# Last stage of a two-layer transformer kernel: head weights held stationary, new bank and queue orders, and the decay mask applied by GpSimd

## What is computed

```python
def _mlstm_parallel(q, k, v, i_pre, f_pre):            # per block and head
    lf = concatenate([0, cumsum(log_sigmoid(f_pre))])
    log_d = lf[1:, None] - lf[None, 1:] + i_pre[None, :]
    log_d = where(t >= s, log_d, -inf)
    m = max(log_d, axis=-1)
    s_mat = (q @ k.T / sqrt(DH)) * exp(log_d - m)
    denom = maximum(abs(sum(s_mat, -1)), exp(-m)) + 5e-5
    return s_mat @ v / denom
# then per head: h * rsqrt(mean(h*h) + 1e-6) * gain, x = x + h
# second half of the layer, on n = layernorm(x):
gate = softmax(n @ gate_w.T); base = n @ weight.T      # 8 experts, rank 16
out = x + base + (sum over experts of gate * (n @ U) @ V) / 16
```

## Time and profile before

| | us |
|---|---|
| median of 3 runs | 431.02 |
| lowest, highest | 430.0, 435.96 |
| profiled execution, its own time | 433.9 |
| span of the profiled execution | 432.0 |
| mean granted TensorE clock | 0.916 |

### The profile page before, as it was taken

How to read it: one execution, slowest core, us unless ns; L and a number is a source line. 1 busy time by engine, 2 the same in 40 slices (tenths; PEclk the granted TensorE clock), 3 DMA queues, 4 the chain that set the end, 5 groups by cost and what they waited for, 6 DMA issues and landing times.

```text
span 432.0 us, 9170 instructions
## 1 busy us (share of the span) xinstructions
PE 344.1 (80%) x3130; PEld 244.1 (57%) x3137; DVE 306.4 (71%) x1028; ACT 248.9 (58%) x470; POOL 185.1 (43%) x209
## 2 busy tenths in 40 slices
PE   2995698989999999824667776677489999999775
PEld 2774566767677777502445554355356666666422
DVE  3897454778898987676999999951537777787641
ACT  1564424664545545726788988874446666666520
POOL 2115200121212345149999999971004555445520
PEclk9999869999999999955999999989579999999965
DMA  7499999988476540000000000000001122212000
GB/s 242 136 281 281 273 303 289 242 167 150 95 148 112 127 71 2 1 0 0 2 1 2 0 2 1 2 0 2 0 14 27 37 51 50 50 39 39 24 25 24
DMA packets 48045, 35.78 MB, mean 83 GB/s; under 512 B 20096, under 2 KB 44032, under 8 KB 47872
## 3 DMA queue, kind: packets, MB, share of 16 engines
q1 hardware_dynamic: 48000, 35.20, 34.1%
HBM read 26.80 MB, written 8.39 MB: 81 GB/s over the span
## 4 chain that ended last, share of the span: by engine, by line
PE 53%; DVE 17%; issue 12%; ACT 5%; POOL 5%; DMA 3%; SPq 3%; DVEq 0%; POOLq 0%; ACTq 0%
PE PS L1438 6%; PE PS L1227 4%; PE PS L1216 4%; PE PS L1246 4%; DVE sm L736 4%; PE PS L1285 4%; PE PS L1428 4%; PE PS L1207 4%; PE PS L1206 4%; PE PS L1405 3%; DMA scr_k<-kpart 3%; PE PS L1423 2%; ACT pT L990 2%; SPq L315 2%; DVE sm L712 2%
## 5 line engine op out<-in xcount | busy, mean ns | idle before, releaser
L990 ACT ACTIVATE pT<-PS 128x512 f32<-128x512 f32 x64 | 36.6, 596 | 49.5 <-PE PS L1207 49.3
L605 DVE TENSOR_REDUCE negm<-PS 128x4 bf16<-128x512 f32 x64 | 42.4, 684 | 15.5 <-PE PS L1216 15.4
L434 POOL TENSOR_TENSOR sm<-sm,mhalf 128x1 f32<-128x1 f32 x16 | 11.3, 708 | 93.0 <-DVE sm L637 93.0
L450 POOL TENSOR_TENSOR kst<-kst,rows 128x1024 f32<-128x1024 f32 x16 | 37.6, 2351 | 5.0 <-ACT kst L1055 4.9
L464 POOL TENSOR_TENSOR kst<-kst,rows 128x1024 f32<-128x1024 f32 x16 | 37.8, 2365 | 0.0
L1320 PE MATMUL PS<-identf,w2f 128*128 128x128 f32 x128 | 19.2, 298 | 23.2 <-ACT w2f L1044 23.0
L1207 PE MATMUL PS<-identb,negm 128*128 128x128 bf16 x256 | 35.6, 222 | 0.0
L1227 PE MATMUL PS<-pT,vx 128*32 128x128 f32 x512 | 27.3, 287 | 5.0 <-ACT pT L990 5.0
L1320 PEld LDWEIGHTS PS<-identf,w2f 128*128 128x128 f32 x128 | 15.1, 151 | 27.7 <-ACT w2f L1044 22.4
L1438 PE MATMUL PS<-wd,xT 128*128 128x392 f32 x64 | 27.7, 560 | 1.8 <-DVE rest L884 1.8
L484 POOL TENSOR_TENSOR smd<-smd,mhalf 128x1 f32<-128x1 f32 x16 | 8.8, 550 | 44.9 <-DVE smd L915 44.9
(11 more groups left out here) (225 smaller groups left out, 1002.6 us busy)
## 6 DMA issues: line engine op xcount, KB each, us to landing
scr_q<-qpart SPq DMA_DIRECT2D x8, 384.0 KB, 4.9
scr_k<-kpart SPq DMA_DIRECT2D x8, 384.0 KB, 6.0
rows<-in_rows SPq DMA_DIRECT2D x1, 2056.0 KB, 11.3
X<-in_x SPq DMA_DIRECT2D x8, 256.0 KB, 4.7
CTXT<-in_ctxT SPq DMA_DIRECT2D x8, 256.0 KB, 4.6
cTb<-in_ctxT SPq DMA_DIRECT2D x16, 128.0 KB, 4.3
vx<-in_ctx SPq DMA_DIRECT2D x16, 128.0 KB, 2.7
out<-rest SPq DMA_DIRECT2D x16, 128.0 KB, 1.7
```

The lines of the kernel that those rows point to most:

```text
L450: gp.tensor_tensor(n2[q.slot], n2[q.slot], ln2g, ALU.mult).then_inc(b_g2, 1)
L605: v.tensor_reduce(negm[f.slot % 2][:, 4 * hg:4 * hg + 4], PS[:, 2 + hg % 2, :].rearrange("p (h k) -> p h k", h=4), AX_X, ALU.max, negate=T ...
L990: s.activation(pT[:, hg, :], PS[:, hg % 2, :], ACT.Exp, scale=float(DH0) ** -0.5).then_inc(a_e, 1)
```

## The change

It touches the last stage only (and the constant `maskb` that it used).

- TensorE: the product of a head takes `smT` (128x128) as the stationary operand and moves the 33 columns of `vx2`, straight into token-by-value form in bank 6. It moves from block a to block b, that is one turn later, and to the head of the turn. The four transposes and ScalarE's copy `yTc` are gone. The two mask matmuls are gone; the log-decays' 512-column matmul comes first. `nd` is transposed into bank 0, `gt` into bank 1; the low-rank product has half a bank of its own (bank 1, columns 256 to 512).
- The order on TensorE becomes: product (b), transposes of `nd` (e), transpose of `gt` (d), scores (a), product with `wd` (e), low-rank product (d), `log_d(0)`, `log_d(1)` (n). `log_d(1)` waits for the output add of d, since both use bank 1.
- ScalarE: `yc`, `xT`, `hsq`, `gtT`, `nd`, `eD`, then both exps.
- GpSimd: two `affine_select` a turn, in place on `dT`, set the masked decays to zero after the exp; the weights wait for these (`c_k`).
- VectorE: first c (heads, X, statistics), then the norm chain of b in one piece, the weights of a, the gate maximum of e, the output add of d, then reciprocal and `gt` of e and a new add, base = bank 7 + X into `outb` (`d_bs`). The output add then adds the low-rank half bank to `outb`.

```diff
@@ constants on GpSimd
-            step(gp.memset(maskb[:], 0.0))
-            step(gp.affine_select(out=maskb[:], in_=maskb[:], compare_op=ALU.is_ge, fill=-30000.0, base=0,
-                                  pattern=[[1, 128]], channel_multiplier=-1))
@@ GpSimd
+            def turn_cd(n, _a, b, c, _e, _d):
+                def masked(half):
+                    pool.wait_ge(c_d, n.b * 2 + half + 1)
+                    d3 = dT[half].rearrange("p (j t) -> p j t", j=4)
+                    gp.affine_select(out=d3, in_=d3, compare_op=ALU.is_ge, fill=0.0, base=0,
+                                     pattern=[[0, 4], [1, 128]], channel_multiplier=-1).then_inc(c_k, 1)
...
+                if n:
+                    masked(0)
+                    masked(1)
@@ VectorE (the order: c, b, weights(a), then)
-                    dve.wait_ge(c_d, a.b * 2 + n + 1)
+                    dve.wait_ge(c_k, a.b * 2 + n + 1)
...
+                if a:
+                    weights(0)
+                    weights(1)
+                if e:
+                    k2.start(e)
+                    dve.wait_ge(d_m, e.b + 1)
+                    v.tensor_reduce(ngm[:], PS[:, 7, D + ER:NM], AX_X, ALU.max, negate=True).then_inc(d_mx, 1)
                 if d:
...
+                    dve.wait_ge(d_l, d.b + 1)
+                    dve.wait_ge(d_bs, d.b + 1)
+                    v.tensor_tensor(outb[d.slot % 2], PS[:, 1, 256:512], outb[d.slot % 2], ALU.add).then_inc(d_o, 1)
+                if e:
...
+                    v.tensor_tensor(outb[e.slot % 2], PS[:, 7, 0:D], X[:, e.b, :], ALU.add).then_inc(d_bs, 1)
@@ ScalarE (the order: yc, xT, hsq, gtT, nd, eD, exp, exp)
-                    act.wait_ge(c_t4, b.b + 1)
+                    act.wait_ge(c_pv, b.b + 1)
...
-                    s.activation(yTc[:], PS[:, 6, :], ACT.Copy).then_inc(c_yT, 1)
@@ TensorE, log_d
-                    if half == 0:
-                        done(pe, c_y, n, -1)
-                    else:
-                        done(pe, d_xT, n, -3)
+                    if half == 0 and e:
+                        pe.wait_ge(d_xT, e.b + 1)
+                    if half == 1 and d:
+                        pe.wait_ge(d_o, d.b + 1)
...
-                    t.matmul(bank, identb[:], maskb[:].unsqueeze(1).to_broadcast([128, 4, 128]), start=True, stop=False)
+                    t.matmul(bank, APARTS[:, n.used, :], rowsel[:, hs:hs + 4].unsqueeze(2).to_broadcast([128, 4, 128]),
+                             start=True, stop=False)
                     for j in range(4):
...
@@ TensorE, the turn
                 if b:
...
+                    pe.wait_ge(c_ld[b.slot % 2], 16 * (b.b // 2 + 1))
+                    pe.wait_ge(c_sm, b.b * 2 + 2)
+                    done(pe, c_y, b, 0)
+                    for h in range(H1):
+                        last = t.matmul(PS[:, 6, h * (DH1 + 1):(h + 1) * (DH1 + 1)], smT[h // 4][:, (h % 4) * 128:(h % 4 + 1) * 128],
+                                        vx2[b.slot % 2][:, h, 0:DH1 + 1], start=True, stop=True)
+                    last.then_inc(c_pv, 1)
+                if e:
+                    pe.wait_ge(d_n, e.b + 1)
                     exps_read(0)
-                    for i in range(4):
-                        last = t.transpose(PS[:, 0, i * 128:(i + 1) * 128], yTc[:, i * 128:(i + 1) * 128], identf[:])
-                    last.then_inc(c_t4, 1)
+                    for i in range(KC):
+                        last = t.transpose(PS[:, 0, i * 128:(i + 1) * 128], nd[:, i * 128:(i + 1) * 128], identf[:])
+                    last.then_inc(d_t, 1)
+                if d:
+                    pe.wait_ge(d_g, d.b + 1)
+                    exps_read(1)
+                    done(pe, d_o, d, 0)
+                    t.transpose(PS[:, 1, 0:128], gt[:], identf[:]).then_inc(d_gt, 1)
                 if a:
...
                     pe.wait_ge(d_xT, e.b + 1)
-                    done(pe, d_o, e, 0)
+                    done(pe, d_bs, e, 0)
...
+                if d:
+                    pe.wait_ge(d_gT, d.b + 1)
+                    t.matmul(PS[:, 1, 256:512], gtT[:], wlv[:], start=True, stop=True).then_inc(d_l, 1)
+                if n:
+                    log_d(0)
+                    log_d(1)
```

More of the change, by code:

```diff
@@ L239, in build @@
         smT = [lnb[i][:].rearrange("p c t -> p (c t)") for i in range(2)]
-        yTc = sb("yTc", [128, 512]); yc = [sb(f"yc{i}", [128, H1, DH1 + 1]) for i in range(2)]; den = sb("den", [128, H1, 4])
+        yc = [sb(f"yc{i}", [128, H1, DH1 + 1]) for i in range(2)]; den = sb("den", [128, H1, 4])
         hd = [sb(f"hd{i}", [128, D]) for i in range(2)]
@@ L854, in weights @@
                                            op0=ALU.mult, op1=ALU.mult).then_inc(c_sm, 1)
-                if d:
-                    k2.start(d)
-                    dve.wait_ge(d_m, d.b + 1)
-                    v.tensor_reduce(ngm[:], PS[:, 7, D + ER:NM], AX_X, ALU.max, negate=True).then_inc(d_mx, 1)
-                    dve.wait_ge(d_e, d.b + 1)
+                if c:
+                    dve.wait_ge(c_yg, c.b + 1)
+                    dve.wait_ge(c_rr, c.b + 1)
+                    v.tensor_tensor(hv[c.slot % 2], hv[c.slot % 2],
+                                    rr[c.slot % 2][:].unsqueeze(2).to_broadcast([128, H1, DH1]), ALU.mult).then_inc(c_hd, 1)
+                    dve.wait_ge(c_hd, c.b + 1)
+                    v.tensor_tensor(X[:, c.b, :], hd[c.slot % 2][:], X[:, c.b, :], ALU.add).then_inc(c_x, 1)
+                    k1.start(c)
+                    zc = smd[c.slot % 2]
+                    dve.wait_ge(c_x, c.b + 1)
+                    take_wait()
+                    c_bn = k1.mark(v.bn_stats(zc[:, 8:14], X[:, c.b, :]))
+                    dve.wait_ge(d_c1, c_bn)
+                    done(dve, d_r, c, -1)
+                    take_wait()
+                    c_var = k1.mark(v.bn_aggr(zc[:, 0:2], zc[:, 8:14]))
+                    dve.wait_ge(d_c1, c_var)
+                    v.tensor_scalar(zc[:, 4:5], zc[:, 0:1], -1.0, None, ALU.mult)
+                    v.tensor_scalar(zc[:, 2:3], zc[:, 1:2], EPS, None, ALU.add).then_inc(d_w, 1)
+                    k1.end()
@@ new lines, in turn_cd @@
+                if b:
+                    cc.start(b)
+                    yb_l = yc[b.slot % 2][:, :, DH1]
+                    dve.wait_ge(c_y, b.b + 1)
+                    b_neg = cc.mark(v.scalar_tensor_tensor(out=den[:, :, 0], in0=yb_l, scalar=-1.0, in1=EM[:, b.b, :],
+                                                           op0=ALU.mult, op1=ALU.max))
+                    dve.wait_ge(c_ch, b_neg)
+                    b_abs = cc.mark(v.tensor_tensor(den[:, :, 1], den[:, :, 0], yb_l, ALU.max))
+                    dve.wait_ge(c_ch, b_abs)
+                    b_den = cc.mark(v.tensor_scalar(den[:, :, 2], den[:, :, 1], 5e-5, None, ALU.add))
+                    dve.wait_ge(c_sq, b.b + 1)
+                    b_sum = cc.mark(v.tensor_reduce(den[:, :, 0], hsq[b.slot % 2][:].rearrange("p (h e) -> p h e", h=H1),
+                                                    AX_X, ALU.add))
+                    dve.wait_ge(c_ch, b_den)
+                    b_floor = cc.mark(v.scalar_tensor_tensor(out=den[:, :, 3], in0=den[:, :, 2], scalar=1e-6, in1=den[:, :, 2],
+                                                             op0=ALU.mult, op1=ALU.mult))
+                    done(dve, c_rr, b, -1)
+                    dve.wait_ge(c_ch, max(b_sum, b_floor))
+                    v.scalar_tensor_tensor(out=ms[b.slot % 2][:], in0=den[:, :, 0], scalar=1.0 / DH1, in1=den[:, :, 3],
+                                           op0=ALU.mult, op1=ALU.add).then_inc(c_ms, 1)
+                    cc.end()
@@ L1115, in turn_cd @@
                     done(act, d_l, d, 0)
[L1116 to L1124 removed]
+                    s.activation(gtT[:], PS[:, 1, 0:128], ACT.Copy).then_inc(d_gT, 1)
                 if c:
@@ L1129, in turn_cd @@
                                  bias=smd[c.slot % 2][:, 5:6]).then_inc(d_n, 1)
+                if e:
+                    act.wait_ge(d_mx, e.b + 1)
+                    done(act, d_g, e, 0)
+                    s.activation(eD[:], PS[:, 7, D + ER:NM], ACT.Exp, bias=ngm[:], accum_out=esum[:]).then_inc(d_e, 1)
+                if n:
+                    exp(0)
+                    exp(1)
             pipeline(act, NB, 4, 6, turn_cd)
```

130 lines of the change are left out of this document (19 added, 111 removed).

## The result

The changed kernel takes 438.52 us (median of 4 runs, 437.15 to 440.95), the one before 432.72 in the same job (430.0 to 435.96): ratio 1.0126, 95% interval [1.0078, 1.0175]. It is slower by 1.3%, less than the 2% that counts as a difference here, but outside the predicted range of 422.5 to 437, and slower (the interval lies wholly above 1) where 0.8 us less was predicted.

A forecast was written before the change was run, and what follows sets the result against it. TensorE's queue was taken to set the 5.905 us turn, then a loop through all engines. Span 432.0 + 5.2 (turns) - 5.1 (drain) - 0.9 (fill) = 431.2; carried to the median, 430.2 us, range 422.5 to 437.

The forecast's parts named there:

- The turn: Last stage, full turns: 6.38 us instead of 5.905, over eleven turns +5.2 us.
- The loop without holds: Full turn: new loop through all engines, from product to log-decays, takes 5.97 us if GpSimd doesn't hold VectorE.
- the holds: Full turn: GpSimd's select and gain product hold VectorE's add to X and first denominator step, 0.41 us on the loop.
- TensorE's sum: Full turn: TensorE's own work falls from 5.905 to 5.67 us, with the heads' product at 0.11 a pair.
- rival C: Heads' product: weight loads don't hide, 0.138 us a pair, 5.4 us in all, total 435.6; chance 0.12.
- The select: GpSimd, full turn: each 128x512 affine_select takes 0.61 us, hidden as a wait but not as a neighbour of VectorE.
- Rival D: GpSimd's select costs like four small ones, 1.17 us, adding 0.7 a turn, total 438; chance 0.08.
- B: Full turn: GpSimd and VectorE meetings don't cost, turn 5.97 us, total 425.7, or 423 with higher drain clock; chance 0.25.
- A: The main forecast: meetings with GpSimd cost VectorE, turn 6.38 us, total 430.2, own range 427 to 433; chance 0.48.
- The drain: Last turns: low-rank piece leaves the loop and base add enters, 1.7 us saved in each of three turns, -5.1 us.
- The fill: First turn, at the lower clock: two mask matmuls at 0.43 each go, -0.9 us.
- rival E: TensorE's clock falls to 1.2 GHz in full turns, loads alone add 1.76 us a turn, total over 440; chance 0.07.

The follow-up runs named there:

- g_all_dummies: Changed kernel with GpSimd's gain product behind the mean square and unread filler matmuls in TensorE's fill and full turns; ratio 0.9987 to the kernel before.
- g_out_early: Changed kernel with late gain product and filler, plus low-rank product ahead of gate products and output add ahead of weights; ratio 1.0103 to the kernel before.
- x_select_again: Repeat of the kernel before with only the mask products replaced by GpSimd's select; ratio 0.9994 to the kernel before.
- e_all_dummies: Changed kernel with unread filler matmuls in TensorE's waits, five in fill turns and three in full turns; 435.73 us, ratio 1.0066 to the kernel before.
- e_wide64: Changed kernel with each matmul of the heads' product moving 64 columns instead of 33; 439.5 us, ratio 1.0184 to the kernel before.
- e_no_select: Changed kernel without the two selects, the mask left out so its output differs; ratio 1.0063 to the kernel before.
- g_early_bare: Changed kernel with late gain product, low-rank product ahead of gate products, output add ahead of weights, no filler; ratio 1.0138 to the kernel before.
- x_select: Kernel before with only the mask products replaced by GpSimd's select after each exp; ratio 0.9949 to the kernel before.
- x_both: Kernel before, old order, with the select, the low-rank product's own half bank and the base add; ratio 1.0086 to the kernel before.

## Why the prediction was wrong, step by step

**The turn: right, a little short.** 6.48 against 6.38. The loop without holds measured 5.98 against 5.97. The first denominator step was held as said. The term that was short is the holds: 0.50 instead of 0.41 on the loop, since both selects meet VectorE (0.56 for `hd`, 0.79 for the add; I had 0.26 on the add alone). Ten turns of 0.57 are 5.7, with the eleventh 6.3, where I had 5.2.

**TensorE's sum: right within 0.1 us.** 0.109 us a pair against 0.11, so rival C (0.138) is out. In g_all_dummies TensorE has no gap and a turn takes 6.25; less the 0.65 that the same filler took in g_out_early that is 5.60, against 5.67. The Trainium skill ("TensorE: Matmul & The Clock Gate", section "Part 3: Packing small matmuls") would have a full-array load wait for the running matmul; 33 and 64 columns at one pace disagree with it, in this shape.

**The select: right.** 0.61 was said, the mean over all 32 is 0.665. As a wait it is hidden, as a neighbour it isn't. Rival D is out, B too, as the meetings cost what A said. The Trainium skill ("SBUF — State Buffer", section "Who interferes with whom") names the lock; its rule gave 6.38, and the trace agrees within 0.1.

**The drain: the size was right, the reason for the rest wrong.** -7.5 against -5.1. x_select_again drains in the old order at a granted clock of 0.93 and takes 24.6; e_all_dummies in the new one at 0.91 takes 19.9. The order is thus worth 4.7, near 5.1; the other 2.8 come from the clock, 0.72 in the drain of before and 0.88 after. That the total came so near is in part luck: the prediction let the last block's own piece stand, but the last gap between output adds fell from 4.86 to 2.44 us in these two profiles, while the first of the last four grew from 5.61 to 6.26.

**The fill: the step that failed first.** I put down -0.9, for the mask products alone; it was +5.1. With the clock kept (e_all_dummies) +2.0 remain, up to 0.5 of them the filler's own: -0.85 up to the first scores (1.80 us from the first log-decays instead of 2.65, the saving that I had put down), +0.7 and +1.2 in the second and third turn (5.31 and 5.77 against 4.59 and 4.60), +1.05 in the fifth, which is a full one already (6.95 against 5.90). In the second and third run paths that I never walked in the fill. Timeline of e_all_dummies there:

```profile
317.98 0.17 DVE L887 SCALAR_TENSOR_TENSOR den<-yc,EM 128x8 f32<-128x8 f32 x1 [3.02 <-ACT yc L1100]
319.38 0.17 DVE L902 SCALAR_TENSOR_TENSOR ms<-den 128x8 f32<-128x8 f32 x1
319.49 1.29 DVE L856 SCALAR_TENSOR_TENSOR lnb<-PS,lnT 128x512 f32<-128x512 f32 x2
319.64 1.64 POOL L491 TENSOR_TENSOR rr<-ms,mhalf 128x8 f32<-128x8 f32 x1 [0.93 <-DVE ms L902]
321.38 0.78 DVE L865 TENSOR_TENSOR hd<-hd,rr 128x256 f32<-128x256 f32 x1 [0.59 <-POOL rr L491]
322.19 0.73 DVE L868 TENSOR_TENSOR X<-hd,X 128x256 f32<-128x256 f32 x1
322.96 0.42 DVE L873 BATCH_NORM_STATS2 smd<-X 128x6 f32<-128x256 f32 x1
323.77 0.28 DVE L887 SCALAR_TENSOR_TENSOR den<-yc,EM 128x8 f32<-128x8 f32 x1
325.01 1.29 DVE L856 SCALAR_TENSOR_TENSOR lnb<-PS,lnT 128x512 f32<-128x512 f32 x2
```

In the second turn the denominators wait for `yc` (3.02), and the next weights stand behind them: product, `yc`, norm chain and weights, parts of the prediction's loop, take it up. In the third the mean square releases GpSimd's root (1.64), VectorE's multiply waits for it, then come add and statistics, and only behind them, without a wait of their own, the next denominators, mean square and weights. In full turns the gate work of e and d lies in that wait and hides it; in the fill there is none. The old order had the weights ahead of all this.

**The clock: the step that failed by kind.** I gave rival E 0.07 because the new product "leaves TensorE occupied" for 5.67 of 6.38 us, and looked at full turns alone. The rows show it falling at 322.0, in the fill, after TensorE had waited 1.72 us for the weights (they end at 321.17), and again at 383.4, after a wait of 1.07 us, longer than the usual 0.72:

```profile
321.27 2.93 PE L1394 MATMUL PS<-vx,lnb 128*128 128x33 f32 x16 [1.72 <-issue]
...
327.57 3.60 PE L1394 MATMUL PS<-vx,lnb 128*128 128x33 f32 x16 [0.38 <-issue]
...
381.72 0.38 PE L1378 MATMUL PS<-rowsel,APARTS 128*128 128x512 bf16 x1 [1.07 <-DVE rest L915]
...
386.33 2.98 PE L1420 MATMUL PS<-wd,xT 128*128 128x392 f32 x4
```

At 1.2 GHz the product takes 3.60 instead of 1.92, as the loads double, and the four gate products 2.98 instead of 1.58. The two turns around 383.4 took 7.62 and 8.26: with 6.48 for each that is 2.9 too much. Rival E named the right thing, but not its place and size: the clock fell for one stretch of the fill and one of the middle, not for all turns.

**The sum again.** By order: fill +2.0, middle +5.7 and 0.2 for one longer turn (most kernels have one near block 11, 0.1 us in the kernel before and 0.35 in e_all_dummies), drain -4.7, together +3.2. By the clock: +3.1, +2.4, -2.8, together +2.7. That is the 5.9 of the stage. Predicted were -0.9, +5.2 and -5.1 by order, and nothing by the clock. Of the 6.7 us between that and the measured stage, the fill's order makes 2.9, the middle's 0.7, the drain's 0.4, and the clock 2.7. The split is that of single profiles.

**What stays open.** What the clock cost in the median execution, and whether the long waits ahead of its falls are their cause. Which stretch falls differs from kernel to kernel: in the middle it fell in the changed kernel, e_wide64, e_no_select and g_early_bare, and not in the others. The share of the product's form in all this was not undone alone, as the old form needs the transposes and their places back. What makes one turn near block 11 longer wasn't looked for either.

## What to carry to other kernels

When an order is written anew, walk its loops in the fill as well as in the full turn: the work that hides a wait in full turns isn't there yet. Before costing what an engine saves, measure how far the other loops are behind it, and what the work that replaces the saving adds to them. Here they were about 0.13 and 0.17 us behind, the select lengthened the second, and 0.44 us of removed matmuls bought 0.085. A faster drain and a longer turn traded against each other here. And TensorE's clock fell in the fill only where TensorE had been left waiting longest, so a new gap in its work may cost more than its length.

## What the runs showed of the hardware

- A matmul of 33 or 64 columns behind a 128x128 f32 load costs 0.109 us a pair; the load paces it, and 31 more columns changed nothing (turn 6.50 against 6.48 us). At the lower clock 16 pairs took 3.60 us instead of 1.92.
- `affine_select` over 128x512 f32 in place takes 0.64 us alone and 1.40 for two back to back; 128x128 took 0.292.
- A VectorE operation with two SBUF operands that meets a GpSimd one ends some 0.28 us after it when it normally takes 0.42 (before: the earlier trace rows); even a step of 8 columns a partition (0.17) was held to 0.52.
- In x_select and x_both `eD` on ScalarE starts 0.51 us behind an activation with scale and bias over 128x256 f32 in SBUF (`nd`, recorded at 0.60).
- Filler matmuls on TensorE kept its clock in the profile of one kernel and not in two others (longest wait left in the fill 0.84 against 1.38 us), and cost 0.1 us a turn where TensorE had too little slack for them.
